# Factor of the back-transformation in 64-column products, with the root taken inside it and the scan rows sent first

## What the reference computes

```
deg = sum(A, -1); d_isqrt = rsqrt(deg)
Lap_norm = d_isqrt[:, None] * (deg * eye - A) * d_isqrt[None, :]
_, U = eigh(Lap_norm)                       # 64 matrices of 128 x 128
agg = einsum('bmn,bmd->bnd', U, features)
h = relu(agg @ W0.T + b0); out = h @ W1.T + b1
ret = einsum('bnm,bmo->bno', U, out)
```

## Time and profile before

| what | value |
|---|---|
| median of three runs | 6235.88 us |
| the profiled execution's own time | 6238.06 us |
| its span in the trace | 6235.6 us |
| TensorE matmul / weight load busy | 2528.0 us (41%) / 1636.1 us (26%) |
| VectorE busy | 4778.0 us (77%) |
| ScalarE / GpSimd busy | 1724.1 us (28%) / 81.4 us (1%) |
| mean granted TensorE clock | 0.667 of full |

### The profile page before, as it was taken

One profiled execution on the slowest core, in us unless ns is written; L12 is line 12 of the kernel. 1 busy time (PEld: TensorE's weight loads), 2 busy tenths in 40 slices (PEclk: granted clock), 3 DMA queues, 4 the chain that ended last, 5 costly groups with the idle time before them and its releaser, 6 DMA issues.

```text
span 6235.6 us, 61923 instructions
## 1 busy us (share of the span) xinstructions
PE 2528.0 (41%) x16242; PEld 1636.1 (26%) x16242; DVE 4778.0 (77%) x19142; ACT 1724.1 (28%) x6552; POOL 81.4 (1%) x45
## 2 busy tenths in 40 slices
PE   1545444444329173471918115601069400100089
PEld 0212112222215141331506114501057400100066
DVE  4666666666689999999985797598978599899812
ACT  0000000000132323313214112327534344324245
POOL 0000000000000000000000000000010000000000
PEclk9666666655558577685859557855589755555599
DMA  5000000000000000000010200310000200200021
GB/s 121 12 14 27 15 15 16 17 19 21 24 16 14 7 14 7 7 7 8 0 14 14 49 0 7 76 27 0 0 7 15 103 0 0 94 0 0 0 68 41
DMA packets 142053, 140.48 MB, mean 23 GB/s; under 512 B 28445, under 2 KB 128426, under 8 KB 134826
## 3 DMA queue, kind: packets, MB, share of 16 engines
q1 hardware_dynamic: 141738, 136.97, 8.0%
HBM read 110.43 MB, written 26.41 MB: 22 GB/s over the span
## 4 chain that ended last, share of the span: by engine, by line
DVE 56%; PE 29%; DMA 6%; ACT 4%; issue 3%; SPq 1%; DVEq 0%; POOL 0%; ACTq 0%; PEldq 0%; POOLq 0%
PE psum L1898 7%; DVE big_b L1043 4%; PE psum L1556 3%; DVE gvec L362 2%; DMA big_b<-rows_dram 2%; ACT big_a L2008 2%; PE psum L1918 2%; PE psum L1611 1%; PE psum L1617 1%; DVE big_a L1053 1%; DVE big_a L1051 1%; PE psum L1615 1%; DVE big_b L1041 1%; DVE big_b L1047 1%; DVE big_b L1046 1%
## 5 line engine op out<-in xcount | busy, mean ns | idle before, releaser
L1898 PE MATMUL psum<-big_a 128*32 128x508 f32 (+59 forms) x4032 | 445.7, 613 | 39.4 <-ACT big_a L1861 39.4
L2066 PE MATMUL psum<-big_b 128*128 128x128 f32 x384 | 71.7, 372 | 844.7 <-ACT big_b L1984 844.7
L2076 PE MATMUL psum<-plane,big_b 128*128 128x128 f32 x192 | 36.0, 366 | 816.7 <-DVEq L1186 800.3
L1505 PE MATMUL psum<-plane,big_a 128*128 128x128 f32 x192 | 49.9, 428 | 650.6 <-ACT big_a L1421 628.6
L2008 ACT ACTIVATE big_a<-big_a 128x128 f32<-128x128 f32 (+1 forms) x896 | 241.8, 271 | 238.8 <-DVE big_a L1053 163.6
L2066 PEld LDWEIGHTS psum<-big_b 128*128 128x128 f32 x384 | 69.4, 284 | 847.0 <-ACT big_b L1984 847.0
L1864 ACT COPY big_a<-psum 128x64 f32<-128x64 f32 x126 | 33.4, 265 | 895.2 <-PE psum L1904 895.2
L2076 PEld LDWEIGHTS psum<-plane,big_b 128*128 128x128 f32 x192 | 32.0, 192 | 818.9 <-issue 800.9
L1556 PE MATMUL psum<-big_b 128*128 128x512 f32 x544 | 244.3, 611 | 0.0
L1043 DVE RECIPROCAL big_b<-big_b 128x512 f32<-128x512 f32 x70 | 234.7, 3353 | 2.4
L355 DVE TENSOR_TENSOR dot_parts<-psum,plane 128x8 f32<-128x8 f32 (+6 forms) x109 | 20.8, 191 | 274.7 <-PE psum L1898 274.7
(11 more groups left out here) (695 smaller groups left out, 10027.9 us busy)
## 6 DMA issues: line engine op xcount, KB each, us to landing
big_a<-rows_dram SPq DMA_DIRECT2D x4, 4096.0 KB, 12.2
vt<-pairs_dram SPq DMA_DIRECT2D x504, 32.0 KB
big_a<-rows_dram SPq DMA_DIRECT2D x4, 2048.0 KB, 17.2
big_a<-rows_dram SPq DMA_DIRECT2D x2, 3072.0 KB, 19.1
big_b<-rows_dram SPq DMA_DIRECT2D x2, 3072.0 KB, 25.9
big_b<-adj SPq DMA_DIRECT2D x2, 2048.0 KB, 17.5
big_b<-adjT SPq DMA_DIRECT2D x2, 2048.0 KB, 39.2
lap_dram<-big_b SPq DMA_DIRECT2D x4, 1024.0 KB, 11.2
```

Of the source, the lines that this page charges most:

```text
L1505: ins = t.transpose(psum[0:parts, bank, g * N:(g + 1) * N], src(g), ident)
L1898: ins = t.matmul(psum[i * SPAN:i * SPAN + MW, 0, 0:4 * wide], v_masked[:, i, q * MW:(q + 1) * MW], anode[:, g:g + 4, k + 1:N + 2 * u], sta ...
L2066: ins = t.matmul(bank(4, g), deflate[:, g, :], w_full[:, g, :], start=True, stop=True)
L2076: ins = t.transpose(bank(0, g), sec[:, g, :], ident)
```

## The change

- The factor's start: ScalarE copies one half of the identity into yT, GpSimd adds the other half of it to the first corner (a third whole-tile instruction beside its two), and TensorE gets y from yT by 16 transposes. The products L1598 to L1602 go. The semaphore is `y_first`.
- GpSimd cuts the corner of s = 2 as well (`ACT_MASKS = 3`), and no longer waits for y before it.
- Steps 1 to 5: only 64 of each 128 columns are computed. m, the addition of y, and yT * m have 64 columns per graph (256 for a bank's product with the identity). The new half of yT is no longer built by products with m, but by multiplying y, as stationary operand, with a 64-column choice from the identity, once y is copied. ScalarE's copies have half the columns. In step 6 only m and the second product are halved.
- The root at levels 0 and 1, which have one turn, is taken by ScalarE inside the turn, in front of its copies of step 5. At level 2 it stays behind both turns.
- SyncE: for the last turn of each level the wait for `turn_ready` and the store move behind the load of the first scan rows; there SyncE then waits until the store has landed, and only then loads the pole rows.

```diff
-            t.wait_ge(S("level_ready"), 7 * q + 1)
+            t.wait_ge(S("y_first"), 2 * q + 2)
             for b in each:
-                t.matmul(psum[:, b, :], ident, four_flat(q_n0, b), start=True, stop=False)
-                t.matmul(psum[:, b, :], ident, over(ident, FB, 1), start=False, stop=True).then_inc(S("yT_ps"), 1)
-                t.matmul(psum[:, 4 + b, :], ident, over(ident, FB, 1), start=True, stop=False)
-                for g in of:
-                    ins = t.matmul(pg(4 + b, g), q_n0[:, 4 * b + g, :], ident, start=False, stop=g == FB - 1)
-                ins.then_inc(S("y_ps4"), 1)
+                transposes(t, b, lambda g: q_yT[:, 4 * b + g, :], S("y_ps4"))
...
                     for g in of:
-                        ins = t.matmul(pg(b, g), level[:, 4 * b + g, :], q_y[:, 4 * b + g, :], start=True, stop=True)
+                        ins = t.matmul(half_bank(b)[:, g, :], level[:, 4 * b + g, :], first[:, 4 * b + g], start=True, stop=True)
                     ins.then_inc(S("ly_ps"), 1)
                 for b in each:
                     t.wait_ge(S("m_ready"), 24 * q + 4 * s + b - 3)
-                    t.matmul(psum[:, 4 + b, :], ident, four_flat(q_y, b), start=True, stop=False)
+                    if s < 6:
+                        t.matmul(psum[:, 4 + b, 0:FB * HALF], ident, fours(first, b), start=True, stop=False)
+                    else:
+                        t.matmul(psum[:, 4 + b, :], ident, four_flat(q_y, b), start=True, stop=False)
                     for g in of:
-                        ins = t.matmul(pg(4 + b, g), q_yT[:, 4 * b + g, :], q_m[:, 4 * b + g, :], start=False, stop=g == FB - 1)
+                        onto = half_bank(4 + b)[:, g, :] if s < 6 else pg(4 + b, g)[:, 0:HALF]
+                        ins = t.matmul(onto, q_yT[:, 4 * b + g, :], q_mh[:, 4 * b + g, :], start=False, stop=g == FB - 1)
                     ins.then_inc(S("y_ps4"), 1)
-                    if s < 6:
-                        t.matmul(psum[:, b, :], ident, four_flat(q_yT, b), start=True, stop=False)
+                if s < 6:
+                    for b in each:
+                        t.wait_ge(S("y_ready"), 28 * q + 4 * s + b + 1)
                         for g in of:
-                            ins = t.matmul(pg(b, g), q_m[:, 4 * b + g, :], q_yT[:, 4 * b + g, :], start=False, stop=g == FB - 1)
+                            ins = t.matmul(half_bank(b)[:, g, :], q_y[:, 4 * b + g, :], second, start=True, stop=True)
                         ins.then_inc(S("yT_ps"), 1)
...
+                if s == root_at:
+                    take_root()
...
+                if s == 0:
+                    p.tensor_tensor(side_of(q_yT, 0, 1), side_of(level, 0, 1), side_of(over(ident, FG, 1), 0, 1), ALU.add).then_inc(S("y_first"), 1)
...
+                    a_turn(a, TURNS[lev][0], 5, lambda: root(base + 1, sc_w[:, 11:13, :]))
...
-                    sy.wait_ge(S("turn_ready"), 4 * q + 4)
-                    sy.dma_start(turned[:, at, :], q_out).then_inc(S("turn_stored"), 16)
+                    if q != TURNS[lev][-1]:
+                        sy.wait_ge(S("turn_ready"), 4 * q + 4)
+                        sy.dma_start(turned[:, at, :], q_out).then_inc(S("turn_stored"), 16)
...
                     rows_from(row_tiles[:, 0:4], slice(0, 4), 0, "scan_rows_in")
+                    if i == 0:
+                        sy.wait_ge(S("turn_ready"), 4 * q + 4)
+                        sy.dma_start(turned[:, at, :], q_out).then_inc(S("turn_stored"), 16)
+                        sy.wait_ge(S("turn_stored"), 16 * q + 16)
                     rows_from(row_tiles[:, 4:7], slice(4, 7), 0, "pole_rows_in")
```

More of the change, by code:

```diff
@@ L1579, in t_front @@
                     ins.then_inc(S("gates_ps"), 1)
-        ACT_MASKS = 2
+        ACT_MASKS = 3
+        q_mh = q_m.rearrange("p g n -> p (g n)")[:, 0:FG * HALF].rearrange("p (g n) -> p g n", g=FG)
+        half_bank = lambda b: psum[:, b, 0:FB * HALF].rearrange("p (g n) -> p g n", g=FB)
+        grouped = lambda ap, s: ap.rearrange("p g (b h) -> p g b h", h=1 << s)
         side_of = lambda ap, s, t: ap.rearrange("p g (b t h) -> p g b t h", t=2, h=1 << s)[:, :, :, t, :]
@@ L1595, in t_turn @@
                 ins.then_inc(S("gram_ps"), 1)
-            t.wait_ge(S("level_ready"), 7 * q + 1)
+            t.wait_ge(S("y_first"), 2 * q + 2)
             for b in each:
-                t.matmul(psum[:, b, :], ident, four_flat(q_n0, b), start=True, stop=False)
-                t.matmul(psum[:, b, :], ident, over(ident, FB, 1), start=False, stop=True).then_inc(S("yT_ps"), 1)
-                t.matmul(psum[:, 4 + b, :], ident, over(ident, FB, 1), start=True, stop=False)
-                for g in of:
-                    ins = t.matmul(pg(4 + b, g), q_n0[:, 4 * b + g, :], ident, start=False, stop=g == FB - 1)
-                ins.then_inc(S("y_ps4"), 1)
+                transposes(t, b, lambda g: q_yT[:, 4 * b + g, :], S("y_ps4"))
             for s in range(1, 7):
                 level = q_n1 if s % 2 else q_n0
+                first, second = side_of(q_y, s, 0), side_of(ident.unsqueeze(1), s, 1)[:, 0]
                 t.wait_ge(S("level_ready"), 7 * q + s + 1)
@@ L1642, in a_mask, with a_turn @@
             ins.then_inc(S("level_ready"), 1)
-        def a_turn(a, q):
+        def a_turn(a, q, root_at=0, take_root=None):
             each = range(4)
@@ L1669, in a_turn @@
                     if s < 6:
[L1670 to L1672 removed]
+                        a.copy(fours(side_of(q_y, s, 0), b), grouped(half_bank(4 + b), s)).then_inc(S("y_ready"), 1)
                     else:
@@ L1677, in a_turn @@
                         ins.then_inc(S("y_ready"), 1)
+                if s < 6:
+                    for b in each:
+                        a.wait_ge(S("yT_ps"), 20 * q + 4 * s + b - 3)
+                        a.copy(fours(side_of(q_yT, s, 1), b), grouped(half_bank(b), s)).then_inc(S("yT_ready"), 1)
             for b in each:
@@ L1691, in p_turn @@
                 level, ups = q_n1 if s % 2 else q_n0, over(pl[f"upper{s}"], FG, 1)
-                if s == 2:
-                    p.wait_ge(S("y_ps4"), 28 * q + 4)
-                elif s > 2:
+                if s > 2:
                     p.wait_ge(S("ly_ps"), 24 * q + 4 * (s - 2))
@@ L1973, in _ @@
                 subs, width = GS[lev] * PAIR[lev] // GB, GS[lev] * PAIR[lev]
-                for q in TURNS[lev]:
-                    a_turn(a, q)
-                root(base + 1, sc_w[:, 11:13, :])
+                if len(TURNS[lev]) > 1:
+                    for q in TURNS[lev]:
+                        a_turn(a, q)
+                    root(base + 1, sc_w[:, 11:13, :])
+                else:
+                    a_turn(a, TURNS[lev][0], 5, lambda: root(base + 1, sc_w[:, 11:13, :]))
                 base += 1
```

13 lines of the change are left out of this document (5 added, 8 removed).

## The result

The changed kernel's first four runs took 6140.11, 6271.54, 6271.84 and 6141.86 us beside a median of 6237.95 for the kernel before (four runs). The ratio of 0.9846 (95% interval 0.9825 to 0.9867) compares the two runs at 6140 to 6142 alone with the kernel before. The other two are runs of the same kernel, and no run of the kernel before had such a second level, so both levels are told of here. Of nine runs three are 1.5% faster than before and six are 0.5 to 0.7% slower.

A forecast was written before the change was run, and what follows sets the result against it. VectorE, busy 4778 of 6236 us, was taken as the bound, so only its waits (141.3 us for the root) could be won; +3 + 7 + 19 = +29 on 6238.06, less 2.2 to the median, gave 6265 us, range 6108 to 6325.

The forecast's parts named there:

- level 0, by L1013: Merge entry at level 0 with a slow turn: root early but pole rows late, +3 us.
- level 1, beyond that: Merge entry at level 1 with a slow turn: pole rows land later, +7 us.
- level 2, beyond that: Level 2: turn 2 slow, 49 us later, turn 3 fast, 35.2 less; +14 at the root, +19 with the store.
- A narrow product costs what a full one did: Steps 1 to 5: a 64-column product priced at 0.112 us like a 128-column one, because weight loads set the pace.
- A fast turn: Turn at full clock, from step 1 to L929: steps of 12.4 us, 84.5 us in all.
- a slow one: Turn at 1.2 GHz: steps 1 to 5 of 23.9 us, 153 us in all, +42.8.
- the -9.5 and +6.3 of the forecast: Start of the factor: step 1 begins 9.5 us earlier in turn 3 and 6.3 us later in turn 2.
- the one on the clock: Clock stays at 1.2 GHz in turns 0 to 2, whose transposes precede a pause, and climbs in turn 3.
- rival 1: Fast in all turns: level 0 -65, level 1 -5, level 2 -48, together -118, 6118 us; chance 0.36.
- The likeliest case: The forecast itself, turns 0 to 2 slow and turn 3 fast: 6265 us, from 6245 to 6285; chance 0.40.
- the 5.4 us: Level 2: GpSimd's third corner slows VectorE by 5.4 us before it wants the root.
- The rule on the clock that I weighed: Rule tying throttle release to TensorE being busy; by it new steps run at full clock and rival 1's time results.

The follow-up runs named there:

- again: The changed kernel once more, with no edit; one run at 6273.60 us.
- primed: Changed kernel plus wide identity products before the transposes and between transposes and step 1; ten runs, four at 6246 to 6258, six at 6305 to 6325 us, ratio 1.0068.
- primed_late: Changed kernel plus six wide products right before step 1 of each turn, behind the wait for its corner; 6142.27 us, ratio 0.9841.
- pause_after: Changed kernel with six wide products before step 1, which then also waits for the s = 2 corner, a pause in turn 2; 6210.98 us, ratio 0.9951.
- kernel after: The changed kernel as first measured and traced; the profiled execution took 6140.11 us.
- again2: The changed kernel, no edit, four more runs: 6147.76, 6269.94 (traced), 6272.13 and 6283.04 us.
- narrow_only: Changed kernel with the root back behind the turns and SyncE's old order; ten runs, 6194 to 6199 (four), 6251 to 6271 (four), 6311 to 6314 us (two).
- late_transposes: Changed kernel with the transposes held back until the s = 1 corner is cut, no wide products; seven runs, 6240 to 6318 us, trace at 6275.
- placed5_few: Changed kernel, three wide products before step 1, root inside the turn only at level 0 (step 5), SyncE's stores moved again; 6115.06 us, ratio 0.9794.
- wide_factor: Kernel before, its 128-column factor kept, with the root inside the turn at levels 0 and 1 and SyncE's new order; 6206.40 us, ratio 0.9941.

## Why the prediction was wrong

Change of VectorE's entry into each merge (L1013) against the kernel before, in us:

| | forecast | run at 6140 | run at 6273.6 |
|---|---|---|---|
| level 0, by L1013 | +3 | -53.3 | -46.2 |
| level 1, beyond that | +7 | +4.8 | +3.2 |
| level 2, beyond that | +19 | -43.0 | +81.2 |
| the rest | 0 | -6.3 | -2.5 |

**What held.** A narrow product costs what a full one did: steps begin 12.4 us apart at full clock and 23.9 at half, both as computed from the earlier trace rows; L1627's 32 take 3.57 us. The prediction took the section "Back-to-back issue gap" of the Trainium skill, "TensorE: Matmul & The Clock Gate", as a rule against this. Its formula by moving columns is for a product by itself; for a stream of loads and products the section says that both set the spacing, and the trace's 0.112 us for either width agrees with that. A fast turn lasts 85.3 us from step 1 to L929 (4705.4 to 4790.7; forecast 84.5), a slow one 146.3 (4774.4 to 4920.7 in `again`; forecast 153, since step 6's second half was faster). From GpSimd's first clearing to step 1 it is 10.4 us in turn 3 (19.9 before) and 26.9 in turn 2 (20.7 before), the -9.5 and +6.3 of the forecast; the addition in turn 2 took 11.12 us, beside VectorE's L787 of 8192 columns (11.28 us). Pole rows held the merge at the turn's end + 22 and + 38 (forecast 24 and 38), the store cost 5.5 at level 2 (forecast 5). Level 1 came out near the forecast: turn 1 slow, the root met on time, VectorE waiting for the turn.

**The step that failed** is the one on the clock: "that it does not climb in turns 0 to 2, whose transposes are followed by a pause, and that it does in turn 3". The mechanism behind it, that a pause in front of the narrow steps loses the clock, holds: primed, primed_late and pause_after show it, and so does the clock inside the pauses of turns 1 and 2 (the short stretches above). What failed is the rest of the step: which turns have a pause, and that transposes without one bring the clock up. The runs showed turn 0 at 1.00 in all five traces with the transposes alone in front of it, and turn 3 at 0.50 in three of the four that have its start as changed. In particular:
- Turn 0 has next to no pause: none in the kernel after, 0.35 to 0.41 us in again, again2 and narrow_only. I had put step 1 at 3301.7. It began at 3296.8: the level had begun 3.1 us earlier, and GpSimd's multiplication took 2.8 us where I had taken the 4.6 of the first one, so that the corner was ready just as the transposes ended. The clock was up from then on; in late_transposes it came up 1 us into step 1. It makes level 0 56 us better than forecast. It is not the full 65 of rival 1, because ScalarE's wait for VectorE in front of step 5 stopped TensorE for 5.19 us, and the stretch from 3356.8 to 3380.0 behind it reads 0.50.
- Turn 3 does not climb surely. Without any pause it was high in one of four traces that have its start as changed (after; not in again, again2, narrow_only), and turn 2 was high in that one too. Nor do Gram products lie right before its transposes, as the prediction has it: TensorE stood 8.33 us between the two, and the transposes took 3.68 us (1.97 at full clock, in primed).
- I gave each turn one outcome. A stream of narrow steps stays for the rest of its turn at the level that it has when step 2 begins, unless it is stopped, so that the outcome of turns 2 and 3 makes 131 us. The likeliest case should have been two numbers.
- That `again` ends near the forecast is luck: level 0 came out 49 us better and level 2 62 us worse than forecast, and the two nearly cancel.

A smaller term: the 5.4 us by which VectorE should come later to the root at level 2 are 6.5 in the trace (from the start of L787 to where it wants the root: 217.8 us before, 224.4 after), 2.5 of it in L789 beside GpSimd's third corner (8.69 and 11.16 us).

The rule on the clock that I weighed (the Trainium skill, "TensorE: Matmul & The Clock Gate", Part 1, by which busyness releases the throttle) would have given turns at full clock. The stretch of turn 1, busy 125.69 of 125.70 us at 0.50, contradicts it in that form, as the earlier trace rows did.

**What stays open.** Why turn 0 came up in every trace and turn 3 in few, though both have 16 transposes, at most 0.4 us of pause behind them and 8 to 10 us of idle time ahead, no run here tells. Nor is it shown why turns 2 and 3 went together in the changed kernel, or what brought turn 2 up at 4600.6, in the midst of step 1. Stops in the middle of a turn are on better ground: all seven of 1.74 us or more, for the root in front of step 5, lost the clock (1.74 in placed5_few, 5.10 to 5.19 in after, again and again2, 36.9 to 40.1 in turn 1 of primed_late, pause_after and late_transposes), and one of 0.44 us in turn 0 of late_transposes did not.

## What to carry to other kernels

When an edit thins out what TensorE does per instruction, ask at which clock the thinner stream begins and what stands right in front of it; if the clock can end up at either level, put a few wide products behind the last wait and in front of the stream (here three, 2.8 us at full clock), not ahead of the wait. Time such a kernel in many runs before trusting a gain: this one is 1.5% faster or 0.5 to 0.7% slower by the same code. And a stream that is bound by its weight loads gains nothing from fewer moving columns; what was won here came from products that went away (some 45 us in the best runs of narrow_only, 6196 beside 6241) and from sending rows while the factor still ran (35 us, wide_factor).

## What was not expected of the hardware

- One and the same stream of fp32 products of 64 columns, TensorE busy throughout, ran for 125 us at a granted clock of 0.50 and for 50 to 66 us at 1.00, with no change from either level, once past step 1, as long as nothing interrupted it (stretches above).
- With this stream behind it, a pause of 1.74 us was enough to fall from the upper level, and one of 0.44 us was not. The length of a pause alone does not tell: the kernel before makes pauses of 2.05 us between products of 128 columns and reads 1.00 throughout (3794.0 to 3821.4).
- The granted clock can rise behind the work and fall with no work at all: in turn 2 of the kernel after it reads 0.50 during the transposes, 1.00 from 4580.3 to 4583.5 and 0.50 again from 4583.7, the last two while TensorE stood still.
- No trace shows this stream climb by itself once it was past step 1 (turn 2 of the kernel after climbed inside step 1); a fall in mid-turn was made good only in step 6, where 512-column products come again.
- More work on TensorE did not mean a higher clock: primed gives it more wide products than the kernel after, and its trace has the lower mean granted clock (0.634 against 0.653).
